# Reordering the start of an attention and expert block: maxima run 4, 4, 5, 6, 7 units ahead, low parts on GpSimd

## What is computed

```python
qkv = cond(x) @ w_qkv.T                      # per batch: [512, 384]
q, k = rope(q), rope(k)                      # 16 heads of 8
scores = einsum('bhsd,bhtd->bhst', q, k) / sqrt(8)
scores = where(causal, scores, -inf)
attn = softmax(scores)                       # max, exp, sum
x = x + einsum('bhst,bhtd->bhsd', attn, v) @ w_out.T
x = x + ffn(experts(x))                      # not touched
```

## Time and profile before

| | |
|---|---|
| median of 3 runs | 181.37 us (180.86 to 181.63) |
| the profiled execution's own time | 180.98 us |
| its span, first to last instruction | 179.1 us |
| PE busy | 168.9 us (94%) |
| DVE busy | 138.9 us (78%) |
| ACT busy | 134.3 us (75%) |
| POOL busy | 93.8 us (52%) |
| granted TensorE clock, mean | 0.998 of full speed |

### The profile page before, as it was taken

One profiled execution on the slowest core, in us unless ns is written; L12 is line 12 of the kernel. 1 busy time (PEld: TensorE's weight loads), 2 busy tenths in 40 slices (PEclk: granted clock), 3 DMA queues, 4 the chain that ended last, 5 costly groups with the idle time before them and its releaser, 6 DMA issues.

```text
span 179.1 us, 3278 instructions
## 1 busy us (share of the span) xinstructions
PE 168.9 (94%) x943; PEld 116.8 (65%) x944; DVE 138.9 (78%) x444; ACT 134.3 (75%) x224; POOL 93.8 (52%) x117
## 2 busy tenths in 40 slices
PE   6899999899999999988999999996999989999992
PEld 2656575565666666653758767864687867788881
DVE  5588989989898899980586999699799658637551
ACT  3569177688768888889734787953879999999970
POOL 5508088985463969688532522021769931676000
PEclk9999999999999999999999999999999999999999
DMA  4824775676686567520110899960760000001001
GB/s 144 294 46 107 191 203 159 218 234 213 166 267 208 143 194 194 164 94 5 62 51 17 231 345 344 347 178 4 241 230 0 0 4 0 0 2 59 0 4 59
DMA packets 15349, 24.28 MB, mean 136 GB/s; under 512 B 2844, under 2 KB 4828, under 8 KB 15308
## 3 DMA queue, kind: packets, MB, share of 16 engines
q1 hardware_dynamic: 14532, 23.29, 42.2%
q10 hardware_dynamic: 800, 0.79, 1.7%
HBM read 18.71 MB, written 5.27 MB: 134 GB/s over the span
## 4 chain that ended last, share of the span: by engine, by line
PE 70%; DVE 11%; ACT 7%; issue 6%; POOL 4%; DVEq 0%; ACTq 0%; POOLq 0%
PE psum L1407 11%; PE psum L1540 10%; PE psum L1541 9%; PE psum L1542 9%; PE psum L1467 8%; PE psum L1443 7%; PE psum L1286 3%; PE psum L1338 2%; PE psum L1352 2%; ACT t_probs L1105 2%; DVE psum L772 2%; DVE t_raw L924 1%; PE psum L1402 1%; ACT t_q_pad L1155 1%; PE psum L1447 1%
## 5 line engine op out<-in xcount | busy, mean ns | idle before, releaser
L772 DVE CUSTOM_DVE_ANT_0 psum<-psum,t_causal 128x128 f32<-128x128 f32 (+3 forms) x128 | 58.6, 525 | 5.8 <-PE psum L1407 3.0
L1105 ACT ACTIVATE t_probs<-psum 128x1024 f32<-128x1024 f32 (+2 forms) x48 | 40.9, 883 | 8.2 <-PE psum L1443 5.2
L1407 PE MATMUL psum<-t_stacked,t_q_pad 96*128 96x256 f32 (+2 forms) x104 | 33.3, 391 | 0.5 <-DVE t_row_max L772 0.2
L1407 PEld LDWEIGHTS psum<-t_stacked,t_q_pad 96*128 96x128 f32 x104 | 18.4, 189 | 12.4 <-DVE t_row_max L772 10.2
L672 POOL TENSOR_SCALAR_AFFINE_SELECT t_probs<-t_probs 128x512 f32<-128x512 f32 x32 | 20.5, 651 | 9.0 <-ACT t_probs L1105 9.0
L944 DVE SCALAR_TENSOR_TENSOR t_q_pad<-psum,t_zw_all,t_q_pad 128x512 fp32r<-128x512 f32 x24 | 17.8, 748 | 9.3 <-ACT t_q_pad L1153 9.2
L1139 ACT ACTIVATE psum<-psum 128x512 f32<-128x512 f32 x40 | 23.4, 586 | 0.9 <-PE psum L1542 0.3
L703 POOL TENSOR_TENSOR t_q_pad<-t_raw,t_q_pad 128x512 fp32r<-128x512 f32 x8 | 10.8, 1357 | 21.0 <-ACT t_q_pad L1155 21.0
L1467 PE MATMUL psum<-t_probs,t_v_all 128*32 128x512 f32 (+3 forms) x256 | 20.6, 439 | 0.0
L772 DVE DVE_READ_ACCUMULATOR2_ANT t_row_max<- 128x1 f32 x128 | 18.0, 141 | 0.0
L1153 ACT ACTIVATE t_q_pad<-psum,t_zw_all 128x512 fp32r<-128x512 f32 x24 | 16.5, 688 | 1.2 <-PE psum L1542 0.6
(11 more groups left out here) (233 smaller groups left out, 369.6 us busy)
## 6 DMA issues: line engine op xcount, KB each, us to landing
t_stacked<-scratch SPq DMA_DIRECT2D x16, 256.0 KB, 5.7
t_probs<-in_L_ffn_Wa SPq DMA_DIRECT2D x2, 1024.0 KB, 11.5
scratch<-t_o_sb SPq DMA_DIRECT2D x7, 256.0 KB, 2.1
t_raw<-in_experts SPq DMA_DIRECT2D x7, 256.0 KB, 3.6
t_stacked<-scratch SPq DMA_DIRECT2D x9, 192.0 KB, 3.7
t_q_pad<-scratch SPq DMA_DIRECT2D x28, 48.0 KB
scratch<-t_dn_hi SPq DMA_DIRECT2D x2, 512.0 KB, 3.4
t_q_two<-scratch SPq DMA_DIRECT2D x5, 192.0 KB, 2.6
```

The costliest lines, as they stand in the source:

```text
L772: last = V.tensor_tensor_reduce(scores, scores, causal[:, S - width:S], 1.0, 3 * BIG, ALU.add, ALU.max, row_max[s][:, qb, j:j + 1])
L1105: A.activation(o, scores, ACT.Exp, scale=float(1.0 / np.sqrt(np.float32(HD)))).then_inc(exp_done, 1)
L1407: last = T.matmul(bank[:, o:o + width], q_pad[s][0:TOP, j, qb * P:(qb + 1) * P], stacked[0:TOP, n, 0:width], start=True, stop=True)
```

## The change

1. `LEAD` = 7 becomes `LEADS` = (0, 4, 4, 5, 6, 7, 7, 7), the units of group n that are done ahead of group n-1's stage. `max_units` puts the rest of group n+1 in the first slices and the lead of group n+2 in the others. Group 0's stage then holds 8 + 4 = 12 units, group 1's 7 + 5 = 12, group 2's 6 + 6 = 12, group 3's 5 + 7 = 12; from group 4 on all is as before.
2. The low parts of batch 0's second half are made by GpSimd instead of VectorE. GpSimd's clearing of `max_pad[0]` moves behind that of `k_pad[0]`. On VectorE each rotation is followed by its sum at once, and the clearing of ones rows (`q1_zero`, the memset of 8x1024) moves from after the first scaling of `xc` to before it.
3. TensorE: the first half's stacking comes before batch 1's `modulate`; group 0's units 0 to 3 follow; then the second half's stacking; then the other units with `project_v(0)` in two halves behind units 4 and 5 and `project(0, t)`, one matmul each, behind units 8 and 10; `project(1, 0)` and `project(1, 1)` around `lay_max_under_q(0)`. `project_v(1)` moves from before group 0's stage into it, behind slice 1. `keep_warm` stands only ahead of units 1, 2 and 3.
4. ScalarE: `modulated(1, ...)` moves behind all eight `place_q0`, `copy_qm(0)` before the second `copy_projection`, the spill of batch 0's keys ahead of the constants and `copy_v(0)`.
5. GpSimd: `spread_last_queries(0)` and `turn(1)` move to right behind `turned(0)`, ahead of group 0's first masking; `turn(0)` no longer waits for `m_ready`; `turned(1)` comes behind the first masking.
6. SyncE: both halves of `pad_k(0)` come behind `pad_q(1)` and `load_k(1)`. The pattern is loaded as 32 rows instead of 128, the constants without the mask, which has a load of its own as before.

```diff
-LEAD, FIRST = 7, 4
+LEADS = (0, 4, 4, 5, 6, 7, 7, 7)
+FIRST = LEADS[1]
...
-    first, end = units_to(n + 1, LEAD if n else FIRST), units_to(n + 2, LEAD)
-    return MX_LIST[first + (end - first) * i // SLICES:first + (end - first) * (i + 1) // SLICES]
+    rest = MX_LIST[units_to(n + 1, LEADS[n + 1]):units_to(n + 2)] if n + 1 < GROUPS else []
+    lead = MX_LIST[units_to(n + 2):units_to(n + 2, LEADS[n + 2])] if n + 2 < GROUPS else []
+    mine, i, k = (rest, i, (len(rest) + 5) // 2) if i < (len(rest) + 5) // 2 else \
+                 (lead, i - (len(rest) + 5) // 2, SLICES - (len(rest) + 5) // 2)
+    return mine[len(mine) * i // k:len(mine) * (i + 1) // k]
...
-            sp.wait_ge(pads_zero, 1)
-            pad_k(0, (0,))
             sp.wait_ge(spilled_1[0], 16 * SPILLS)
             sp.wait_ge(q1_zero, 1)
             pad_q(1)
             sp.wait_ge(spilled_1[1], 16 * SPILLS)
             load_k(1)
-            pad_k(0, (1,))
+            sp.wait_ge(pads_zero, 1)
+            pad_k(0)
...
-            pool.wait_ge(lo_ready, 4)
+            pool.wait_ge(lo_ready, 2)
+            for i in range(2):
+                pool.wait_ge(hi_ready, 3 + i)
+                G.tensor_tensor(qk_lo[:, i, S2:S], roped[:, i, S2:S], f32_of(qk_hi[:, i, S2:S]),
+                                ALU.subtract).then_inc(lo_ready, 1)
...
             turn(0)
             turned(0)
+            spread_last_queries(0)
+            turn(1)
...
                     if n == 0 and c == 0:
-                        turn(1)
-                    if n == 0 and c == 1:
-                        spread_last_queries(0)
                         turned(1)
...
             V.tensor_scalar(dvar[:], QM[:, 0:B], 1e-8, None, ALU.add).then_inc(dvar_ready, 1)
+            V.memset(f32_of(stacked[TOP:ROWS, 0:GROUPS, 3 * P:S]), 1.0).then_inc(q1_zero, 1)
...
-            for h in range(2):
-                if h:
-                    dve.wait_ge(ld_rotb, 16)
-                rotate(0, h)
-                rotate(1, h)
-                add_turned(0, h)
-                add_turned(1, h)
-                take_low(0, h)
-                take_low(1, h)
+            for i in range(2):
+                rotate(i, 0)
+                add_turned(i, 0)
+            take_low(0)
+            take_low(1)
+            dve.wait_ge(ld_rotb, 16)
+            for i in range(2):
+                rotate(i, 1)
+                add_turned(i, 1)
...
-            modulated(1, xc[:, 1, :], psum[:, 2, :])
             place_q0(0, 0)
             copy_k0(0)
+            place_q0(1, 0)
             take_hi_half(0, 1)
-            place_q0(1, 0)
+            place_q0(2, 0)
             take_hi_half(1, 1)
-            place_q0(2, 0)
             place_q0(3, 0)
             copy_q0(0)
+            place_q0(0, 1)
             copy_k0(1)
-            for j in range(HG):
+            for j in range(1, HG):
                 place_q0(j, 1)
...
+            modulated(1, xc[:, 1, :], psum[:, 2, :])
+            copy_q0(1)
+            spill(act, 2, NG, 1, spilled)
...
+            copy_v(0)
             copy_projection(0)
-            copy_q0(1)
-            copy_v(0)
-            spill(act, 2, NG, 1, spilled)
+            copy_qm(0)
             copy_projection(1)
-            copy_qm(0)
...
-                if n == 0 and u not in (0, 7):
+                if n == 0 and u in (1, 2, 3):
                     keep_warm(1, bank)
...
-            modulate()
-            keep_warm(FILL[0])
             stack_half(0, 0)
             stack_half(1, 0)
-            project(0)
-            scores_for_max(0, 0)
+            modulate()
+            for u in range(HG):
+                scores_for_max(0, u)
             stack_half(0, 1)
             stack_half(1, 1)
-            for u in range(1, len(MX_UNITS[0])):
+            scores_for_max(0, 4)
+            project_v(0, (0, 1))
+            scores_for_max(0, 5)
+            project_v(0, (2, 3))
+            for u in range(6, len(MX_UNITS[0])):
                 scores_for_max(0, u)
-                if u == 6:
-                    project_v(0)
-            project(1)
+                if u in (8, 10):
+                    project(0, u // 2 - 4)
             scores_for_max(1, 0)
             scores_for_max(1, 1)
+            project(1, 0)
             lay_max_under_q(0)
-            project_v(1)
+            project(1, 1)
...
                 maximum(1)
+                if n == 0:
+                    project_v(1)
                 maximum(2)
```

More of the change, by code:

```diff
@@ L596, in _ @@
             G.memset(causal[:, 0:S - P], 0.0).then_inc(causal_zero, 1)
-            G.memset(max_pad[0][:], 0.0).then_inc(pads_early, 1)
             pool.wait_ge(ld_cond, 32)
@@ L603, in _ @@
             G.memset(f32_of(k_pad[0][0:TOP]), 0.0).then_inc(pads_zero, 1)
-            pool.wait_ge(lo_ready, 4)
+            G.memset(max_pad[0][:], 0.0).then_inc(pads_early, 1)
+            pool.wait_ge(lo_ready, 2)
[3 more added lines that the diff above has]
+                                ALU.subtract).then_inc(lo_ready, 1)
             G.memset(v_all[:], 1.0).then_inc(v_ones, 1)
@@ L623, in turn @@
                 pool.wait_ge(pj_copied, i + 1)
-                if i == 0:
-                    pool.wait_ge(m_ready, 1)
                 for t, o in enumerate((rope_c[i], rope_s[i])):
@@ L757, in add_turned, with take_low @@
                                 ALU.add).then_inc(roped_ready, 1)
-            def take_low(i, h):
-                dve.wait_ge(hi_ready, 2 * h + i + 1)
-                V.tensor_tensor(qk_lo[:, i, half(h)], roped[:, i, half(h)], f32_of(qk_hi[:, i, half(h)]),
+            def take_low(i):
+                dve.wait_ge(hi_ready, i + 1)
+                V.tensor_tensor(qk_lo[:, i, half(0)], roped[:, i, half(0)], f32_of(qk_hi[:, i, half(0)]),
                                 ALU.subtract).then_inc(lo_ready, 1)
@@ L957, in add_residual @@
                 V.tensor_tensor(y[:, b, :], MISC if b else OUT, x12[:, b, :], ALU.add).then_inc(y_ready, 1)
-            V.memset(f32_of(stacked[TOP:ROWS, 0:GROUPS, 3 * P:S]), 1.0).then_inc(q1_zero, 1)
             dve.wait_ge(ld_rota, 16)
-            for h in range(2):
-                if h:
-                    dve.wait_ge(ld_rotb, 16)
-                rotate(0, h)
-                rotate(1, h)
-                add_turned(0, h)
-                add_turned(1, h)
-                take_low(0, h)
-                take_low(1, h)
+            for i in range(2):
[7 more added lines that the diff above has]
+                add_turned(i, 1)
             dve.wait_ge(ld_const, 32)
@@ L1035, in take_sel @@
                 act.wait_ge(ld_sel, 16)
-                A.copy(sel[q, 0, :, :], pattern[q, :].rearrange("p (t m) -> p t m", t=4)).then_inc(sel_ready, 1)
+                A.copy(sel[q, 0, :, :], pattern.rearrange("p (t m) -> p t m", t=4)).then_inc(sel_ready, 1)
             def half(h):
@@ L1340, in project_half, with project, project_v @@
                 last.then_inc(qk_ready, 1)
-            def project(i):
-                pe.wait_ge(xc_ready[2], 1)
-                if i == 0:
-                    pe.wait_ge(rope_ready, 2)
-                    at_ = 0
-                else:
-                    wait_slot("project", i)
-                    at_ = slot_of("project", i)
-                for t in range(2):
-                    last = T.matmul(ST[:, at_ + t, :], w_qk[:, i, t, :], xc[:, 1, :], start=True, stop=True)
-                last.then_inc(qk_ready, 1)
-            def project_v(b):
+            def project(i, t):
+                if t == 0:
+                    pe.wait_ge(xc_ready[2], 1)
+                    if i == 0:
+                        pe.wait_ge(rope_ready, 2)
+                    else:
+                        wait_slot("project", i)
+                T.matmul(ST[:, slot_of("project", i) + t, :], w_qk[:, i, t, :], xc[:, 1, :],
+                         start=True, stop=True).then_inc(qk_ready, 1)
+            def project_v(b, blocks=range(KB)):
                 if b == 0:
@@ L1363, in project_v @@
                 pe.wait_ge(ld_wv, 16)
-                for kb in range(KB):
+                for kb in blocks:
                     last = T.matmul(PV[:, kb * P:(kb + 1) * P], xc[:, b, kb * P:(kb + 1) * P],
                                     w_v, start=True, stop=True)
-                last.then_inc(v_ready, 1)
+                if blocks[-1] == KB - 1:
+                    last.then_inc(v_ready, 1)
             def stack_half(i, h):
@@ L1708, in host_constants @@
     consts = np.zeros((P, C_END), np.float32)
-    consts[:, C_ID:C_MASK] = np.eye(P, dtype=np.float32)
+    consts[:, C_ID:C_HEAD] = np.eye(P, dtype=np.float32)
     k, q = np.mgrid[0:P, 0:P]
-    consts[:, C_MASK:C_HEAD] = np.where(k > q, np.float32(BIG), np.float32(0.0)).T
-    consts[0:TOP, C_HEAD:C_END] = np.arange(TOP)[:, None] // (PARTS * HD) == np.arange(HG)[None, :]
+    consts[:, C_MASK:C_END] = np.where(k > q, np.float32(BIG), np.float32(0.0)).T
```

(1 more changed line is left out.)

19 lines of the change are left out of this document (9 added, 10 removed).

## The result

The changed kernel takes 182.89 us (median of five runs; 182.55 to 182.93) against 181.37 (also five; 180.86 to 181.63): a ratio of 1.0084, 95% interval 1.0065 to 1.0103. It is slower by 1.5 us where 0.7 us less was forecast. The profiled execution took 182.55 us with a span of 180.4, against 180.98 and 179.1.

The account below looks back on a forecast made before the run. TensorE was taken as the bound from group 1's stage on, with VectorE and GpSimd sharing it in group 0's; -1.45 us gained plus 0.7 paid back gave -0.7, from 181.37 to 180.7 us, range 179.3 to 181.9.

Parts of the forecast that it names:

- What bounds the kernel: From group 1's stage on TensorE, an extra matmul costing its full time; group 0's stage bound by TensorE, VectorE and GpSimd.
- Part 1: The first 22 us: first maximum at about 12.95, group 0's maxima done at 21.1 instead of 22.12, 1.0 us gained.
- the stated range: Start of the kernel, memset moved before the scaling of xc: 0.1 us of delay taken, range 0 to 0.3.
- the second rival: Start of the kernel: GpSimd's subtraction holds up VectorE's second sum by 0.65 us; -0.2, 181.2 us; chance 0.16.
- The rule that the prediction weighed: VectorE with two SBUF inputs and GpSimd reading SBUF share a port pair; the second is held for the other's whole.
- Part 2: Group 0's stage: GpSimd comes last, m_ready(1) at 31.1, group 1's stage begins at 32.5; gain so far 1.45 us.
- costs nothing here: Group 0's stage: added project_v(1), 0.95 us on TensorE, lies in front of the wait for the first masking.
- Part 3: Stages of groups 1 to 3: one more unit each at TensorE's 0.24 us, 0.7 us back; VectorE still below the stage.
- The third: Stages of groups 1 to 3: lead of 4 too short, TensorE waits for VectorE, up to 0.7 us each; 182.0; chance 0.11.
- The clock: From 16 us on, TensorE might run units and projections at the lower clock level: +2.0, 183.4 us; chance 0.07.

Follow-up runs that it names:

- b_pe: The kernel before with one more zero matmul of 512 columns on TensorE in each of the stages of groups 1 to 3; 181.67 us, ratio 1.0029.
- g_pm: The changed kernel with old leads and slices, turn(0)'s wait for m_ready and the memset's old place, turned(1) behind the placing of group 1's maxima; 181.31 us.
- a_leads: The changed kernel with the old leads and the old even slices; 182.39 us, ratio 1.0048.
- a_both: The changed kernel with the old leads and even slices and turn(0)'s wait for m_ready put back; 181.57 us, ratio 1.0012.
- f_pv2: The changed kernel with old leads and slices, turn(0)'s wait for m_ready, the memset's old place, and project_v(1) behind group 0's third score block; 181.53 us.
- g_best: The changed kernel with old leads, slices, m_ready wait and memset place, turned(1) behind the placing of group 1's maxima, project_v(1) behind maximum(2); 181.65 us.
- b_leads: The kernel before with only the new leads and slices (LEADS and the new max_units); 183.29 us, ratio 1.0099.
- b_early: The kernel before with the new leads and slices, but in groups 1 and 2 the doubled slice ahead of the weighing; 182.44 us, ratio 1.0065.
- b_swap: The kernel before with the paired groups' units over 512 columns made ahead of those over 384; 183.19 us, ratio 1.0091.
- b_dve: The kernel before with one more 384-column mask-and-maximum on VectorE in each of the stages of groups 1 to 3; 181.58 us, ratio 1.0019.
- b_even: The kernel before with the new lead numbers but its old even slices; 185.97 us, ratio 1.0227.
- a_wait: The changed kernel with turn(0)'s old wait for m_ready put back; 182.73 us, ratio 1.0075.

## Why the prediction was wrong, step by step

- **What bounds the kernel.** The rule was wrong. "An extra matmul costs its full time" from group 1 on: `b_pe` says 0.11 to 0.13 a stage for a matmul of 512 columns, half of the 0.24. And a TensorE that reads busy 8.21 of 8.24 us can still be waiting. Its weight loads show one such wait, in the kernel before, where its matmuls show next to none:

```profile
38.94 0.19 PEld L1407 LDWEIGHTS psum<-t_stacked,t_q_pad 96*128 96x128 f32 x1 [0.23 <-DVE t_row_max L772]
```

  The two engines hold each other up by turns, so a sum of one of them does not price a unit.
- **Part 1.** Forecast for the end of group 0's maxima 21.1, measured 21.45. First maximum 13.19 instead of 12.95: the memset did not vanish in the wait for GpSimd, `xc` is scaled at 6.28 instead of 5.96. That is 0.3, the upper end of the stated range, and VectorE got little of it back; with the memset where it was, `g_pm` has its first maximum at 12.94. The idle time ahead of unit 4 was 0.52 (forecast 0.5 to 0.9, start 16.33 for 16.1). GpSimd's subtractions took 0.80 each where I took 0.69. The second sum was not held up (0.42 us at 12.85), so the second rival failed at the place that I gave it.
- **The port, at a place not looked at.** The rule that the prediction weighed did strike, 9 us later. The prediction never costed the removal of `m_ready` from `turn(0)`; it looked like a wait that only delays GpSimd. It also kept GpSimd's product apart from VectorE's subtraction. The rows: 0.18 us alone, 1.14 and 1.15 beside the product, where the earlier trace rows had 0.55 for a product caught by a shorter remainder. The Trainium skill, "SBUF — State Buffer", section "SBUF: two separate sides", says that of two such operations the later one waits for the whole of the earlier; by that rule, the trace agrees. With the old leads it costs 0.7 to 0.8 us (`a_leads` against `a_both`); in the change as made GpSimd's earlier row makes up for it.
- **Part 2.** "VectorE has group 1's maxima done at 29, so GpSimd is the one that comes last": VectorE's last read of them ends at 31.09, GpSimd had been idle for 0.54 us, and its placing starts at 31.22, 0.13 us behind. (The profile names an exponential of ScalarE for that wait, but its row ends at 31.23, too late to be what ended it.) VectorE came last in the kernel before too, and with the same 0.13 us. There its last maximum ran from 29.70, the read of it ended at 30.49, and GpSimd's placing followed at 30.62:

```profile
29.70 0.73 DVE L772 CUSTOM_DVE_ANT_0 psum<-psum,t_causal 128x512 f32<-128x512 f32 x1
```

```profile
30.62 0.20 POOL L644 CAST t_max_pad<-t_row_max 128x16 bf16<-128x16 f32 x1 [0.24 <-issue]
```

  VectorE sets that point, so what delays VectorE in group 0's stage counts in full. The row of GpSimd was well summed (31.1 forecast for the placing's end, 31.7 measured, 0.54 of it waiting). `project_v(1)` "costs nothing here": VectorE loses 0.55 us over it between units 5 and 6 (0.56 in `a_both`), since it had no unit in hand, and `f_pv2` and `g_best` show the cost moving with it. Beside the subtraction this is why nothing of part 1 is left at group 1's maxima: they end 0.60 us later than before. The gain lies behind them, where the prediction put it, and is smaller. The weighing starts at 34.98 for the 34.45 forecast (0.9 us won for 1.45), and group 1's stage 1.09 us earlier, where 1.7 was forecast. What makes that gain takes both halves of the change:

```profile
32.71 1.49 PE L1408 MATMUL psum<-t_stacked,t_q_pad 96*128 96x384 f32 x3
```

```profile
33.30 0.47 PE L1456 MATMUL psum<-t_stacked 104*128 104x512 f32 x1 [0.99 <-POOL t_stacked L662]
```

```profile
32.56 0.55 PE L1410 MATMUL psum<-t_stacked,t_q_pad 96*128 96x384 f32 x2
```

  The first row is `a_both`, where three units for VectorE still stand between `scores_for_exp(0, 5)` and group 1's stage (34.05). The second is `b_leads`, where TensorE waits 0.99 for GpSimd's spreading (33.96, or about 33.5 with the first maximum where the kernel before has it). The third is the kernel after, which has neither (32.95).
- **Part 3, the term that decides, and the step that failed.** 0.24 us a group forecast, 1.13, 0.49 and 0.47 measured: 2.09 in place of 0.7. The prediction priced a unit by TensorE's spacing and took VectorE's 0.5 us as free, since its sum stayed below the stage ("8.0 of 8.5, still below"). It was not free: in groups 2 and 3 the stage grew by VectorE's own 0.48 and 0.52 us, with its idle time nearly as before (0.81 and 0.72 for 0.80 and 0.77). What idle time there is lies where a unit can't use it: the units are handed over in a fixed row through three banks, the weighing takes 1.43 us out of it, and TensorE takes the next unit before its own scores whether or not a bank is free. In group 1's stage the size and place of the units around the weighing add to it: TensorE waits 0.48 us for a maximum, and VectorE is idle 0.31 us more than before. `b_early` and `b_swap` show that place and size alone are worth 0.17 to 0.86 and 0.25 to 0.43 us a stage. How the 1.13 divides among number, size and place isn't shown, as no run put the moved slice into the kernel after.
- **The rivals.** The third, a lead of 4 too short, was the right one: TensorE waits for VectorE right behind the slices that it names (0.48 us in group 1's stage, 0.37 in group 2's), a unit costs VectorE's own time, and the measured 0.7 us a group on average is its upper price. It had 0.11 because VectorE idles 0.8 us per group. That idle time is no room against it: 0.51 us of it lie behind the weighing, where VectorE has nothing in hand. Only the other 0.28 could be filled, as `b_dve` did, and one more unit in the row did not fill it. Its time of 182.0 is still 0.9 us short, for the 0.36 less won at the stage's start, the 0.26 in the FFN and the 0.3 outside the span. The clock did not fall in the change (1.00 in every stage), though it did in `b_even`.
- **The FFN's 0.26 us.** From the start of group 7's stage to the end it is 96.09 us before, 96.04 to 96.08 in `b_leads`, `b_dve`, `b_pe`, `b_early` and `b_swap`, and 96.33 to 96.37 in the kernel after, `a_both`, `a_leads`, `a_wait`, `g_pm`, `g_best` and `f_pv2`. It arises in one step of VectorE: from a small subtraction to the product with the gates that follows it is 0.12 us in the kernel before and these five (131.28 to 131.40 in the kernel before) and 0.38 in the others (132.29 to 132.67 in the kernel after). What an execution takes beyond its span goes the same way, 1.74 to 1.86 us with the old beginning and 1.97 to 2.17 with the new one. Both go with the new beginning, not with leads or wait; the cause stays open, and no run was made for it. In `g_pm` it takes more than half of the 0.44 us that its group 1 starts early.

## What to carry to other kernels

Idle time of an engine is only room for more work if the work can be there when the engine is idle: look at each piece of it, and at what the engine holds in hand as it begins. Where two engines hand units over in a fixed order through few buffers, price one more unit by a run that moves one, not by either engine's sum, and look at the weight loads too before calling TensorE the bound. And a wait that is taken away may have kept two engines apart: ask what will run beside what.

## What the runs showed of the hardware

- A VectorE subtraction of 128x16 elements with both inputs in SBUF takes 0.18 us alone and 1.14 to 1.15 us when a GpSimd product of 128x512 has begun 0.15 us ahead (`after`, `a_leads`); it ends 0.03 to 0.04 us after the product.
- TensorE's granted clock fell to its 1.2 GHz level in `b_even` at about 34.4 us, after two waits of 1.50 and 0.99 us that ended at 32.43 and 34.11, and was back at about 37.8, after 3.4 us of work without a gap. The second wait by itself is no sign of a fall: `b_leads` has one of 0.99 us that ended at 33.30, and its clock stayed at 1.00.

```profile
32.43 0.40 PE L1421 MATMUL psum<-t_minus_ident_b,t_max_pad 128*128 128x128 bf16 x4 [1.50 <-POOL t_max_pad L647]
...
34.11 0.49 PE L1453 MATMUL psum<-t_stacked 104*128 104x512 f32 x1 [0.99 <-POOL t_stacked L659]
```
